# A selective-scan kernel: the last product by C of each scan run moves from GpSimd to VectorE, and TensorE adds it up ahead of turning back the first half

## The chip, the cores and the metric

The kernel runs on one core of one Trainium2 chip. A core has TensorE (PE, matmuls and transposes into PSUM; PEld is its weight load), VectorE (DVE), ScalarE (ACT), GpSimd (POOL) and SyncE (SP), which issues the transfers. Each works through its own instructions in order and waits for the others by semaphores. The metric is the device time of one execution in microseconds (us), as the median of several runs.

## The reference

Four layers run one after the other on x (2 batches, 1024 tokens, 256 channels): a linear attention (layer 0), a gated state-space block (layer 1), a bidirectional state-space block (layer 2) and a softmax attention (layer 3). The change touches the state-space scans of layers 1 and 2 alone. Each is, for 512 channels and 16 states:

```python
def step(hst, inp):
    dt_t, B_t, C_t, x_t = inp
    dA = jnp.exp(dt_t[:, :, None] * A)
    hst = hst * dA + (dt_t * x_t)[:, :, None] * B_t[:, None, :]
    y = jnp.einsum('bds,bs->bd', hst, C_t)
    return (hst, y)
```

Layer 1 has one such scan for each batch, layer 2 has one forward and one backward scan for each batch. y is then multiplied by a gate and goes through an output projection.

## The kernel before

**Runs.** The six scans are six "runs": q = 0 and 1 in layer 1 (batches 0 and 1), q = 2 to 5 in layer 2 (batch 0 forward and backward, batch 1 forward and backward). A run handles two halves of 512 tokens in turn (`r.order`), 16 states in each, 4 groups of 128 channels for each state: 128 units (`UNITS`), or 64 pairs of units (`PAIRS_N`). The pair holds two channel groups of one state: a tile `H` of 128 partitions x 1024 values, of which there are five (`HS`), used in turn.

**One pair.** TensorE forms the input u of a unit in a PSUM bank (L840 or L846). ScalarE makes the decay exp(dt*A) (L931). VectorE scans the unit with one instruction (L1000). When both units of a pair are scanned, GpSimd multiplies the pair in place by the row of C, which a transfer has spread over the partitions (L1019, semaphore `weighed`). TensorE then adds the pair into the y banks with 8 transposing matmuls (`add_up`, L865, semaphore `added`), which sums over the 16 states. The order on each engine is the order in which `run_t`, `run_s`, `run_v` and `run_p` are written.

**The end of a run.** VectorE makes its last scans of units 126 and 127. TensorE adds the pairs 61, 62 and 63. In the runs q = 0, 1, 3 and 5 the function `run_t` is given `back`, which is `turn_back_t`: `back(0)` turns the y of the first half, which has long been copied to SBUF, with 16 transposes into four banks (L1029); `back(1)` does so for the second half. VectorE multiplies each turned bank by the gate (`turn_back_v`, L1036). Between the two it takes the second half's y out of PSUM (`take_y(1)`): in q = 0 and 1 it copies the y banks 0 and 1 (L820) while ScalarE copies banks 2 and 3 (L812); in q = 3 and 5 it adds all four to the forward scan's y (L818). Each bank of `back(1)` needs all four of these parts. TensorE goes on from `back(1)` to the output projection (L265). The runs q = 2 and 4 have no `back`: TensorE goes on to the next run's inputs.

In `run_t`, `back(0)` stands between `add_up(62)` and `add_up(63)`:

```python
            for pair in range(PAIRS_N - 3, PAIRS_N):
                if pair == PAIRS_N - 1 and back:
                    back(0)
                add_up(pair)
```

Of the kernel before, what the change touches and what calls it, by code (L numbers as in the profile page):

```python
# [8 lines left out]
ALU = mybir.AluOpType  # L9
# [102 lines left out]
def program(nc, T, out):  # L112
    with ExitStack() as ctx:
# [5 lines left out]
        def sig(name, step=1):  # L119
            every.append(Sig(ctx.enter_context(nc.semaphore(name)), step))  # L120
            return every[-1]
# [35 lines left out]
        pe, act, dve, pool = sig("psum_filled"), sig("scalar_done"), sig("vector_done"), sig("pool_done")  # L157
        spread, scaled, formed = sig("b_diagonal"), sig("scaled_by_b"), sig("u_formed")
        decayed, scanned, carried = sig("decayed"), sig("scanned"), sig("carried")
        weighed, added = sig("weighed_by_c"), sig("added_up")  # L160
        taken = sig("y_taken")
        dma = {}

        def transfer(name):
            return dma[name]
# [7 lines left out]
        def area(off, *shape):  # L173
            n = 1
            for s in shape:
                n *= s
            assert off + n <= AW, (off, n)
            v = A[:, off:off + n]
            if len(shape) == 2:
                v = v.rearrange("p (a b) -> p a b", a=shape[0])  # L180
            if len(shape) == 3:
                v = v.rearrange("p (a b c) -> p a b c", a=shape[0], b=shape[1])
            return v
# [429 lines left out]
        CB = [area(WK + 7168 + 512 * j, 512) for j in range(2)]  # L613
        w2all = W2[:, 4992:7040]
        UNITS, PAIRS_N, HS = 128, 64, 5
# [109 lines left out]
        def first_state(r, j):  # L725

            return r.G[j], Bt[:, 4 * r.order[0] + j, 0:1], r.q >= 2 and j >= 2
# [23 lines left out]
        def first_copied(r, j):  # L751
            return (dve if first_state(r, j)[2] else act).at(("dut", r.q, 0, j))
# [31 lines left out]
        def second_half(w, r):  # L784

            w.wait_ge(*act.at(("dut", r.q, 1, 3)))
            w.wait_ge(*dve.at(("dut", r.q, 1, 1)))
# [15 lines left out]
        def took(r, p, j):  # L803

            return act.at(("took", r.q, p, j)) if by_scalar(r, p, j) else taken.at((r.q, p, j))

        def by_scalar(r, p, j):
            return r.n < 2 and (p == 0 or j >= 2)
# [13 lines left out]
        def run_t(e, w, r, back=None, early=None):  # L822
            q = r.q
            opened = set()

            def form_u(i):
                k, dt = divmod(i, 4)
                if k < 32:
                    ci = r.steps[k][0]
                    if ci == r.order[1]:  # L830
                        second_half(w, r)
                    if i >= 4:
                        w.wait_ge(*scanned.at((q, i - 4)))
                    else:
                        w.wait_ge(*first_copied(r, i))
                    o = PS[:, 4 + i % 4, :]
                    if k % 2:
                        w.wait_ge(*spread.at((q, k, 3)))
                        for j in range(4):
                            t = e.matmul(o[:, j * 128:(j + 1) * 128], r.DUT[:, 4 * ci + j, dt * 128:(dt + 1) * 128], DB[k // 2 % 2][:, j, :],  # L840
                                         start=True, stop=True)
                    else:
                        for j in range(4):
                            w.wait_ge(*(dve.at(("scaled", q, j)) if k == 0 and first_state(r, j)[2] else scaled.at((q, k, j))))
                        for j in range(4):
                            t = e.transpose(o[:, j * 128:(j + 1) * 128], r.G[(2 * k + j) % 6][:, dt * 128:(dt + 1) * 128], ident[:, :])  # L846
                    t.then_inc(*formed.up((q, i)))

            def open_y(ci, j):

                if (ci, j) in opened:
                    return False
                opened.add((ci, j))
                if ci == r.order[0]:
                    w.wait_ge(*(dve if j < 2 else act).at(("dut", q, 1, j)))
                else:
                    w.wait_ge(*took(r, 0, j))
                return True

            def add_up(pair):  # L860
                ci = r.steps[pair // 2][0]
                w.wait_ge(*weighed.at((q, pair)))
                for dt in (pair % 2 * 2, pair % 2 * 2 + 1):
                    for j in range(4):
                        t = e.matmul(PS[:, j, dt * 128:(dt + 1) * 128], r.H[pair % HS][:, dt % 2, j * 128:(j + 1) * 128], ident[:, :],  # L865
                                     start=open_y(ci, j), stop=True, is_transpose=True, skip_group_check=True)
                t.then_inc(*added.up((q, pair)))

            def add_skip(ci, n):
                dt, j = divmod(n, 4)  # L870
                w.wait_ge(*dve.at(("diag", q)))
                e.matmul(PS[:, j, dt * 128:(dt + 1) * 128], r.U[:, dt, ci * 512 + j * 128:ci * 512 + (j + 1) * 128], diag[:, dt, :],  # L872
                         start=open_y(ci, j), stop=True, skip_group_check=True)

            for i in range(3):
                form_u(i)
            for i in range(UNITS):
                k, dt = divmod(i, 4)
                ci, s = r.steps[k]
                if dt % 2 and i >= 7:  # L880
                    add_up((i - 7) // 2)
                form_u(i + 3)
                if 1 <= i < 5:
                    turn_du_t(e, w, r, 1, i - 1)
                if 3 <= s < 11 and dt % 2:
                    add_skip(ci, 2 * (s - 3) + dt // 2)
            banks.at, banks.held = 4, [[("last y", q, j)] for j in range(4)] + [[("last u", q, j)] for j in range(4)]
            for pair in range(PAIRS_N - 3, PAIRS_N):
                if pair == PAIRS_N - 1 and back:
                    back(0)  # L890
                add_up(pair)
                if pair == PAIRS_N - 3 and early:
                    early()
            if back:
                back(1)

        def run_s(e, w, r, y, more, early=None):
# [76 lines left out]
        def run_v(e, w, r, y, back=None):  # L974
            q = r.q

            def take_y(p):
                for j in range(4):
                    if not by_scalar(r, p, j):
                        take_v(e, w, r, p, j, y)  # L980

            for i in range(UNITS):
                k, dt = divmod(i, 4)
                ci, s = r.steps[k]
                if i == TAKEN_AT:
                    take_y(0)
                if i in (5, 6):
                    copy_du_v(e, w, r, 1, i - 5)
                if i == 6:
                    w.wait_ge(*pe.at(("dut", q, 1, 3)))  # L990
                w.wait_ge(*decayed.at((q, i)))
                w.wait_ge(*formed.at((q, i)))
                if i >= 2 * HS:
                    w.wait_ge(*added.at((q, i // 2 - HS)))
                init = 0.0
                if ci == r.order[1]:
                    w.wait_ge(*carried.at((q, 2 * s + dt // 2)))
                    init = CAR[:, 4 * s + dt:4 * s + dt + 1]
                h, a, u = (v[:, ::-1] if r.rev else v for v in (r.H[i // 2 % HS][:, dt % 2, :], A_B[i % 4], PS[:, 4 + i % 4, :]))
                e.tensor_tensor_scan(h, a, u, init, ALU.mult, ALU.add).then_inc(*scanned.up((q, i)))  # L1000
            if back:
                back(0)
            take_y(1)
            if back:
                back(1)
            for j in range(4):
                banks.give(("last y", q, j), took(r, 1, j))
                banks.give(("last u", q, j), scanned.at((q, UNITS - 4 + j)))

        def run_p(e, w, r):  # L1010
            q = r.q
            for pair in range(PAIRS_N):
                k = pair // 2
                w.wait_ge(*scanned.at((q, 2 * pair + 1)))
                if r.steps[k][0] == r.order[0]:
                    w.wait_ge(*carried.at((q, pair)))
                w.wait_ge(*transfer(f"c_load{k % 2}").at((q, k)))
                h = r.H[pair % HS]
                e.tensor_tensor(h, h, CB[k % 2].unsqueeze(1).broadcast_to([128, 2, 512]), ALU.mult).then_inc(*weighed.up((q, pair)))  # L1019
# [955 lines left out]
```

## Time and profile before

| | |
|---|---|
| median of 3 runs | 1942.12 us |
| range of these runs | 1942.08 to 1942.58 us |
| the profiled execution's own time | 1945.84 us |
| its span, first to last instruction | 1943.5 us |
| busy: PE, DVE, ACT, POOL | 95%, 82%, 73%, 54% |
| POOL's products by C (L1019) | 384 of 2396 ns mean |
| VectorE's scans (L1000) | 768 of 1201 and 1259 ns mean |
| TensorE's additions (L865) | 3072 matmuls |
| mean granted TensorE clock | 0.975 of full speed |

A granted clock of 1.00 is TensorE's level of 2.4 GHz, 0.50 is the level of 1.2 GHz. The busy shares are averages over stages with different limits, so what a change at the end of a run is worth has to be read there: in the chain of waits and in the timeline around each end. Busy time of TensorE is modelled: the matmuls overlap, and a group's end lies a little after the next group's start.

### The profile page before, as it was taken

The numbers are of one execution on the slowest core, as the hardware profiler recorded it, in microseconds if no ns is written. First come the engines' busy times: TensorE is split into PE (matmuls) and PEld (weight loads), VectorE is DVE, ScalarE is ACT, GpSimd is POOL, SyncE is SP. The second block draws the span as 40 slices with busy tenths as digits, with TensorE's granted clock in tenths as the row PEclk, the third lists the DMA queues.
The fourth block names the chain that finished last, engine by engine and source line by source line (L and its number), as shares of the span: only waits on it lengthen the run. The fifth ranks groups of instructions, "written<-read, shape, count | busy, mean of one in ns | idle before, by whom it ended". The sixth has DMA issues, their size and how long they took to land.

```text
span 1943.5 us, 32682 instructions
## 1 busy us (share of the span) xinstructions
PE 1845.3 (95%) x12312; PEld 1337.9 (69%) x12312; DVE 1600.7 (82%) x2125; ACT 1425.8 (73%) x2661; POOL 1048.6 (54%) x603
## 2 busy tenths in 40 slices
PE   6989899999999999999999999999998999999997
PEld 3664899948998599969995799689974333332323
DVE  5565899768998699989995999889987999999742
ACT  3426899468993899799974999799954377777775
POOL 3031599526994299939980699479944400003000
PEclk9989899998999999999999999999999799999999
DMA  5023111021111111101110121021101111111000
GB/s 202 1 85 99 59 57 55 32 72 43 56 59 37 51 54 60 51 24 55 56 44 2 40 60 56 24 72 58 58 15 32 38 42 38 37 37 36 17 23 22
DMA packets 57547, 95.18 MB, mean 49 GB/s; under 512 B 14951, under 2 KB 23559, under 8 KB 55982
## 3 DMA queue, kind: packets, MB, share of 16 engines
q1 hardware_dynamic: 55854, 88.90, 15.2%
q0 software_dynamic: 1536, 4.20, 0.7%
q8 instruction: 97, 1.59, 0.3%
q14 instruction: 60, 0.49, 0.1%
HBM read 73.55 MB, written 6.91 MB: 41 GB/s over the span
## 4 chain that ended last, share of the span: by engine, by line
PE 63%; POOL 14%; ACT 8%; DVE 8%; issue 6%; DMA 1%; SPq 1%; DVEq 0%; ACTq 0%; POOLq 0%
POOL A L1019 13%; PE PS L865 10%; PE PS L840 10%; PE PS L256 8%; PE PS L1603 6%; PE PS L1556 6%; PE PS L1763 5%; PE PS L846 5%; PE PS L265 3%; DVE A L1569 2%; PE PS L441 2%; PE PS L872 1%; ACT A L931 1%; ACT A L908 1%; PE PS L243 1%
## 5 line engine op out<-in xcount | busy, mean ns | idle before, releaser
L1019 POOL TENSOR_TENSOR A<-A 128x1024 f32<-128x1024 f32 x384 | 897.6, 2396 | 223.2 <-ACT small L923 111.0
L931 ACT ACTIVATE A<-A,negA 128x512 f32<-128x512 f32 x768 | 547.3, 715 | 34.0 <-DVE A L1000 24.4
L1000 DVE TENSOR_TENSOR_SCAN A<-A,PS 128x512 f32<-128x512 f32 x384 | 436.2, 1201 | 44.8 <-PE PS L846 23.8
L1000 DVE TENSOR_TENSOR_SCAN A<-A,small,PS 128x512 f32<-128x512 f32 x384 | 451.2, 1259 | 5.3 <-ACT A L931 5.3
L865 PE MATMUL PS<-ident,A 128*128 128x128 f32 x3072 | 408.5, 276 | 20.4 <-ACT A L737 13.3
L840 PE MATMUL PS<-A 128*128 128x128 f32 x3072 | 393.8, 276 | 0.9 <-ACT A L915 0.6
L865 PEld LDWEIGHTS PS<-ident,A 128*128 128x128 f32 x3072 | 352.3, 143 | 30.0 <-ACT A L737 15.9
L840 PEld LDWEIGHTS PS<-A 128*128 128x128 f32 x3072 | 368.1, 192 | 2.3 <-DVE A L1000 2.0
L1569 DVE TENSOR_REDUCE A<-PS 128x1 f32<-128x512 f32 x512 | 319.3, 681 | 38.9 <-PE PS L1556 37.3
L1800 ACT ACTIVATE A<-PS 128x512 f32<-128x512 f32 x512 | 267.2, 603 | 101.9 <-PE PS L1763 101.6
L908 ACT ACTIVATE A<-A,small 128x512 f32<-128x512 f32 x320 | 228.6, 714 | 17.3 <-PE PS L846 16.8
L846 PE MATMUL PS<-ident,A 128*128 128x128 f32 x1360 | 200.4, 279 | 4.5 <-ACT A L737 2.5
L1556 PE MATMUL PS<-A 99*128 99x512 bf16 x480 | 186.6, 397 | 13.7 <-DMA A<-scr 7.5
L256 PE MATMUL PS<-A,W 128*128 128x512 f32 (+1 forms) x416 | 184.8, 598 | 3.3 <-DVE A L766 2.9
L1763 PE MATMUL PS<-A 102*128 102x512 bf16 x480 | 178.1, 384 | 5.1 <-ACT A L1800 4.9
L846 PEld LDWEIGHTS PS<-ident,A 128*128 128x128 f32 x1360 | 162.4, 145 | 8.9 <-issue 4.1
L1534 POOL CAST W<-W 128x32 bf16<-128x32 f32 x32 | 6.7, 209 | 291.4 <-DVE W L1527 214.3
L1556 PEld LDWEIGHTS PS<-A 99*128 99x128 bf16 x480 | 46.9, 98 | 166.5 <-DVE A L1569 121.6
L230 POOL TENSOR_TENSOR RS<-VE,HALF 128x8 f32<-128x8 f32 (+1 forms) x15 | 25.7, 1712 | 248.9 <-DVE VE L225 248.9
L915 ACT ACTIVATE A<-ident,small 128x128 f32<-128x128 f32 x384 | 148.6, 393 | 0.4 <-PE PS L840 0.4
L256 PEld LDWEIGHTS PS<-A,W 128*128 128x128 f32 (+1 forms) x416 | 75.1, 185 | 102.6 <-issue 91.0
L1603 PE MATMUL PS<-A,W 128*32 128x512 f32 x1024 | 136.0, 604 | 0.0
(194 smaller groups left out, 1842.7 us busy)
## 6 DMA issues: line engine op xcount, KB each, us to landing
A<-scrc SPq DMA_DIRECT2D x192, 256.0 KB, 3.1
A<-A SPq DMA_DIRECT2D x360, 32.0 KB
scr<-A SPq DMA_DIRECT2D x4, 1024.0 KB, 4.8
W<-in_wa SPq DMA_DIRECT2D x2, 1536.0 KB, 9.7
X<-in_x SPq DMA_DIRECT2D x4, 512.0 KB, 5.3
scr<-W SPq DMA_DIRECT2D x128, 1.5 KB
out<-X SPq DMA_DIRECT2D x4, 512.0 KB, 2.9
W<-in_w SPq DMA_DIRECT2D x1, 1984.0 KB, 7.3
```

What stands on the lines that cost most here:

```text
L256: t = e.matmul(o[0:M, :], wt(k, m), act_in(k), start=k == 0, stop=k == nk - 1)
L840: t = e.matmul(o[:, j * 128:(j + 1) * 128], r.DUT[:, 4 * ci + j, dt * 128:(dt + 1) * 128], DB[k // 2 % 2][:, j, :], start=True, stop=True)
L846: t = e.transpose(o[:, j * 128:(j + 1) * 128], r.G[(2 * k + j) % 6][:, dt * 128:(dt + 1) * 128], ident[:, :])
L865: t = e.matmul(PS[:, j, dt * 128:(dt + 1) * 128], r.H[pair % HS][:, dt % 2, j * 128:(j + 1) * 128], ident[:, :], start=open_y(ci, j), stop ...
L931: e.activation(A_B[i % 4], r.DT[:, dt, ci * 512:(ci + 1) * 512], ACT.Exp, scale=negA[:, r.n, dt * 16 + s:dt * 16 + s + 1]).then_inc(*decay ...
L1000: e.tensor_tensor_scan(h, a, u, init, ALU.mult, ALU.add).then_inc(*scanned.up((q, i)))
L1019: e.tensor_tensor(h, h, CB[k % 2].unsqueeze(1).broadcast_to([128, 2, 512]), ALU.mult).then_inc(*weighed.up((q, pair)))
L1556: e.matmul(o, SQ[j][0:99, nt * 128:(nt + 1) * 128], SK3[j][0:99, c * 512:(c + 1) * 512], start=True, stop=True).then_inc(*pe.up(("trial", ...
L1569: e.tensor_reduce(NM[:, k % 2, q:q + 1], bank(("trial", k, nt, c)), AX.X, ALU.max, negate=True).then_inc(*dve.up(("trial", k, nt, c)))
L1603: t = e.matmul(PV[32 * j:32 * j + 32, c, :], V[:, tile * 272 + 17 * h:tile * 272 + 17 * h + 32], PX[mt % 2][j][:, c * 512:(c + 1) * 512], ...
L1763: e.matmul(o, SK3[sl][0:102, mt * 128:(mt + 1) * 128], SQ[sl][0:102, c * 512:(c + 1) * 512], start=True, stop=True).then_inc(*pe.up(("scor ...
L1800: e.activation(PX[mt % 2][j][:, c * 512:(c + 1) * 512], bank(key), ACT.Exp).then_inc(*act.up(("weights", u, mt, j, c)))
```

## The change

The last of the 64 products by C leaves GpSimd. VectorE makes it with the same operands right behind the scan of unit 127, in front of its own `back(0)`; it waits for its own last scan and for the transfer of that row of C, and raises a semaphore of its own (`weighed_v`), for which `add_up(63)` now waits. GpSimd makes 63 products in each run. TensorE adds pair 63 right behind pair 62, and makes `back(0)` and `back(1)` after it.

```diff
@@ add_up in run_t
-                w.wait_ge(*weighed.at((q, pair)))
+                w.wait_ge(*(weighed_v if pair == PAIRS_N - 1 else weighed).at((q, pair)))
@@ end of run_t
             for pair in range(PAIRS_N - 3, PAIRS_N):
-                if pair == PAIRS_N - 1 and back:
-                    back(0)
                 add_up(pair)
                 if pair == PAIRS_N - 3 and early:
                     early()
             if back:
+                back(0)
                 back(1)
@@ run_v, behind the loop over the units
+            w.wait_ge(*scanned.at((q, UNITS - 1)))
+            w.wait_ge(*transfer("c_load1").at((q, 31)))
+            h = r.H[(PAIRS_N - 1) % HS]
+            e.tensor_tensor(h, h, CB[1].unsqueeze(1).broadcast_to([128, 2, 512]), ALU.mult).then_inc(*weighed_v.up((q, PAIRS_N - 1)))
             if back:
                 back(0)
@@ run_p
-            for pair in range(PAIRS_N):
+            for pair in range(PAIRS_N - 1):
```

On TensorE, at the end of the run q = 0 (L865 adds pairs, L1029 turns back, and is L1032 in the changed file):

```order
 L865 MATMUL PS<-ident,A 128x128 x8
 L840 MATMUL PS<-A 128x128 x8
-L865 MATMUL PS<-ident,A 128x128 x32
-L1029 MATMUL PS<-ident,A 128x128 x16
-L865 MATMUL PS<-ident,A 128x128 x8
-L1029 MATMUL PS<-ident,A 128x128 x16
+L865 MATMUL PS<-ident,A 128x128 x40
+L1032 MATMUL PS<-ident,A 128x128 x32
```

The 8 additions of pair 63 moved from behind the first 16 transposes to in front of them; nothing else moved. The ends of q = 1, 3 and 5 have the same piece.

On VectorE, at the same place before the change (L1000 the scans, L1036 the gate, L820 the copies of y, L1219 behind the output projection):

```order
142 L1000 SCALAR_TENSOR_TENSOR A<-A,small,PS 128x512 x64
143 L1036 TENSOR_TENSOR A<-PS,A 128x512 x4
144 L820 COPY A<-PS 128x512 x2
145 L1036 TENSOR_TENSOR A<-PS,A 128x512 x4
146 L1219 TENSOR_TENSOR A<-PS,MODS 128x512 x4
```

and with it:

```order
142 L999 SCALAR_TENSOR_TENSOR A<-A,small,PS 128x512 x64
143 L1003 TENSOR_TENSOR A<-A 128x1024
144 L1039 TENSOR_TENSOR A<-PS,A 128x512 x4
145 L820 COPY A<-PS 128x512 x2
146 L1039 TENSOR_TENSOR A<-PS,A 128x512 x4
147 L1222 TENSOR_TENSOR A<-PS,MODS 128x512 x4
```

One product (L1003) stands between the last scan and the gate of the first half.

## Rows read from the trace of the kernel before

**Rows 1.** The page: shares of the chain that ended last, by engine.

```profile
PE 63%; POOL 14%; ACT 8%; DVE 8%; issue 6%; DMA 1%; SPq 1%; DVEq 0%; ACTq 0%; POOLq 0%
```

**Rows 2.** The chain, end of q = 0: start us, us, what.

```profile
363.02 2.37 POOL A L1019
...
365.43 1.09 PE PS L865 x8
...
367.00 2.48 DVE A L1036 x4
369.48 1.21 DVE A L820 x2
...
370.73 1.85 PE PS L1029 x15
372.59 13.82 PE PS L265 x64
```

**Rows 3.** Timeline, end of q = 0: start us, us, engine, line, what, [idle before <-releaser].

```profile
356.05 11.65 POOL L1019 TENSOR_TENSOR A<-A 128x1024 f32<-128x1024 f32 x5
356.90 8.28 DVE L1000 TENSOR_TENSOR_SCAN A<-A,small,PS 128x512 f32<-128x512 f32 x7
...
366.36 1.91 PE L1029 MATMUL PS<-ident,A 128*128 128x128 f32 x16
...
368.11 1.04 PE L865 MATMUL PS<-ident,A 128*128 128x128 f32 x8
...
370.13 0.33 PE L1029 MATMUL PS<-ident,A 128*128 128x128 f32 x1 [0.99 <-DVE A L820]
```

**Rows 4.** Timeline, end of q = 5.

```profile
1413.48 8.29 DVE L1000 TENSOR_TENSOR_SCAN A<-A,small,PS 128x512 f32<-128x512 f32 x7
...
1422.87 1.91 PE L1029 MATMUL PS<-ident,A 128*128 128x128 f32 x16
...
1426.72 0.33 PE L1029 MATMUL PS<-ident,A 128*128 128x128 f32 x1 [1.06 <-DVE A L818]
```

**Rows 5.** The chain, end of q = 5.

```profile
1419.51 2.39 POOL A L1019
...
1423.58 2.48 DVE A L1036 x4
...
1428.51 1.64 PE PS L1029 x13
...
1430.36 1.93 PE PS L265 x8
```

**Rows 6.** The chain, end of q = 3.

```profile
1017.65 2.54 PE PS L1029 x13
...
1020.51 2.50 PE PS L265 x8
```

**Rows 7.** Timeline, start of layer 3: VectorE's and GpSimd's products of 128x1024.

```profile
1462.46 1.22 DVE L1480 TENSOR_TENSOR A<-A 128x1024 f32<-128x1024 f32 x1
...
1465.15 2.50 POOL L1480 TENSOR_TENSOR A<-A 128x1024 f32<-128x1024 f32 x1 [5.32 <-ACT A L1470]
1465.58 3.15 DVE L1480 TENSOR_TENSOR A<-A 128x1024 f32<-128x1024 f32 x1
```

**Rows 8.** Timeline, end of q = 2.

```profile
828.44 1.29 DVE L820 COPY A<-PS 128x512 f32<-128x512 f32 x2 [4.93 <-PE PS L865]
```

**Rows 9.** Timeline, starts of q = 3 and q = 5: TensorE's longest waits there.

```profile
864.20 0.33 PE L865 MATMUL PS<-ident,A 128*128 128x128 f32 x1 [1.89 <-ACT A L737]
...
1276.22 0.33 PE L865 MATMUL PS<-ident,A 128*128 128x128 f32 x1 [1.70 <-ACT A L737]
```

**Rows 10.** Busy time by stretch: us, PE, PEld, DVE, ACT, POOL busy (count), PEclk, DMA share, GB/s.

```profile
864.60:868.00 3.40, 2.32 (x11) 2.33 (x12) 1.53 (x3) 3.25 (x7) 3.04 (x2) 0.50 0.24 82
1018.00:1021.70 3.70, 3.70 (x16) 2.97 (x15) 3.45 (x7) 0.00 (x0) 0.00 (x0) 0.54 0.00 0
```

More of the change, by code:

```diff
@@ L159, in program @@
         decayed, scanned, carried = sig("decayed"), sig("scanned"), sig("carried")
-        weighed, added = sig("weighed_by_c"), sig("added_up")
+        weighed, weighed_v, added = sig("weighed_by_c"), sig("weighed_by_c_on_vector"), sig("added_up")
         taken = sig("y_taken")
```

## The prediction

> **What bounds the kernel now.** I read the page first. The chain that ended last is 63% TensorE and 14% POOL [rows 1], and nearly all of POOL's part is the products by C inside the scan runs. That makes it tempting to think that one POOL product less in a run is 2.4 us less. The change takes only the last of 64 away, though, so what counts is which wait ends last after it. For that I read the chain in order of time around each of the six ends of a run, and then the timeline of the same stretch.
>
> At the end of q = 0 the chain goes: POOL's product of pair 62 (363.02, 2.37 us), TensorE's addition of pair 62 (365.43), the first four transposes of back(0), VectorE's four gate products of the first half (367.00 to 369.48), VectorE's two copies of y, back(1) on TensorE from 370.73, then the output projection, 64 matmuls without a gap [rows 2]. POOL's product of pair 63 is not in it. The timeline shows where that product is: POOL makes pairs 59 to 63 from 356.05 to 367.70, about 2.33 us each [rows 3]. It ends while TensorE is busy with back(0) (366.36, 16 transposes, 1.91 us). TensorE adds pair 63 from 368.11 to 369.15, and VectorE is busy with the gate products until 369.48, so it would not have looked at pair 63 earlier [rows 2, 3]. In the kernel before, both the product and the addition of pair 63 are hidden behind VectorE's gate products, with 0.33 us to spare. q = 1 repeats this. q = 3 and 5 differ only in that VectorE adds four banks instead of copying two; the chain passes through the same POOL product of pair 62 and the same gate products [rows 5].
>
> **The change part by part.**
>
> *POOL's 64th product goes* (six times). It was not on the chain at four ends. At the ends of q = 2 and 4 VectorE sits idle for 4.93 us before it takes y, and what it waits for is TensorE's addition [rows 8], which is behind the next run's first projection, not behind POOL. Worth nothing.
>
> *VectorE's product comes in* (six times). A VectorE product of 128x1024 from SBUF takes 1.22 us when POOL is quiet, and took 3.15 us when POOL's 2.50 us product, begun 0.43 us earlier, was still under way for 2.07 us [rows 7]. So a VectorE product with both operands in SBUF all but stands still while POOL works: POOL's ended at 1467.65, VectorE's at 1468.73, 1.08 us later. Here is the overlap at q = 0: the last scan ends at 365.18 [rows 3] and POOL's pair 62 at 365.39 [rows 2]. Counting 0.04 us from one instruction to the next that waits for it (POOL's end at 365.39 to TensorE's 365.43), the product would run from 365.22 to 366.44 if POOL did not matter, and to 366.61 if it stood still until POOL ends and then took its full 1.22 us. TensorE could begin adding pair 63 at 366.48 to 366.65.
>
> The Trainium skill, page "SBUF — State Buffer", section "SBUF: two separate sides", says that the port pair that VectorE and GpSimd share is an exclusive lock, held for a whole instruction by the one that starts first, also against a VectorE instruction with two SBUF inputs. The trace agrees with its 3.15 us; by that rule the upper value holds, and no more than that, because POOL has nothing behind pair 62. I lean towards the upper value.
>
> *The 8 additions of pair 63 go in front of back(0)* (four times with effect). This is the term that costs. From the addition of pair 62 to the first transpose of back(0) passes 366.36 - 365.43 = 0.93 us [rows 2, 3]; the eight additions of pair 63 will take the same. So back(0) begins at 366.48 + 0.93 = 367.41, or at 366.65 + 0.93 = 367.58, in place of 366.36: 1.05 to 1.22 us later. VectorE's first gate product needs the first four transposes, so it moves from 367.00 by the same amount, and with it the gate products, the copies, back(1) and the projection. VectorE has no slack in that stretch: the gate products, the copies and back(1) follow each other closely [rows 2].
>
> For q = 5: the last scan ends at 1421.77 [rows 4], POOL's pair 62 at 1421.90 [rows 5]. The product ends at 1423.03 to 1423.12, TensorE begins pair 63 at 1423.07 to 1423.16, back(0) at 1424.00 to 1424.09, against 1422.87 [rows 4]: 1.13 to 1.22 us later. Sum over four ends, q = 1 taken as q = 0 and q = 3 as q = 5: 2 x 1.05 + 2 x 1.13 = 4.36 to 4 x 1.22 = 4.88. I take 4.6.
>
> *What is gained by adding pair 63 early?* Its y is complete at about 367.6 instead of 369.15, and ScalarE copies its two banks earlier. VectorE stands in program order before its own gate products of the first half, however, and takes its share of y only after them. back(1) needs all four parts. So the gain is zero.
>
> *TensorE waits longer in one piece.* Before, TensorE had something to do (pair 63) while VectorE made the gate products, and its wait before back(1) was 0.99 us at q = 0 and 1.06 us at q = 5 [rows 3, 4]. After the change back(0) ends at 367.41 + 1.91 = 369.32 and back(1) begins at 370.13 + 1.05 = 371.18: a wait of 1.86 us. At q = 5 the same gives 1424.00 + 1.91 = 1425.91 to 1426.72 + 1.13 = 1427.85: 1.94 us. Elsewhere in this trace TensorE waited 1.89 and 1.70 us in one piece with single matmuls around it, at the starts of q = 3 and q = 5 [rows 9], and behind the first of these the granted clock stood at 0.50, the level of 1.2 GHz, from 864.6 to 868.0 [rows 10]. At the end of q = 3 the clock fell as it is, in the stretch from 1018.0 [rows 10], behind a wait as long as q = 5's, where it did not. What such a fall costs is the difference of those two ends: from the last 13 transposes to the end of the first eight projection matmuls q = 3 took 1020.51 + 2.50 - 1017.65 = 5.36 us and q = 5 took 1430.36 + 1.93 - 1428.51 = 3.78 us [rows 5, 6], so 1.58 us. At q = 0 the projection behind back(1) is on the chain and a fall costs about the same. At q = 1 VectorE's norm is on the chain soon after back(1), so it costs less. Of the three ends that had no fall I expect two to get one, at 1.2 us each (between 1.58 and about half of it for q = 1): 2.4 us. Bounds: no new fall, 0; all three, 3 x 1.58 = 4.7. Below zero too: q = 3 could lose its fall, since every time after 367 us shifts, for -1.6.
>
> **Sum.** In the profiled execution's time 1945.84 + 4.6 + 2.4 = 1952.8 us. That execution is 3.7 us above the median of the runs (1942.12); I know no reason for the change to alter this distance, so the forecast is 1942.12 + 7.0 = 1949.1 us.
>
> **The rivals.**
> 1. *Only the fixed term.* The waits of 1.9 us bring no net fall of the clock: +4.4 to +4.9, 1946.5 to 1947.0 us. For it: a wait of about a microsecond fell once and stayed up once, so chance plays a part. Against it: the new waits are about as long as those of rows 9.
> 2. *Within measurement.* The fixed term holds, but a fall that the kernel has now goes away: 4.6 - 1.6 = +3.0, 1945.1 us.
> 3. *Faster.* If the end of a run hung on pair 63, the earlier product would pay: POOL ends it at 367.70, VectorE would at 366.44 to 366.61, 1.1 to 1.26 us earlier, times four: 1937.1 to 1937.7 us. This decides as soon as pair 63's addition ends later than VectorE's gate products, that is, if the 0.33 us to spare were negative in the unprofiled runs. Even then the additions stand before back(0) now, so the gate products come late all the same. Little speaks for it.
> 4. *VectorE's product is much dearer.* If POOL stood in its way all through, as in the 3.15 us row, each end would cost 1.9 us more: +7.7, 1956.8 us with the forecast's terms. It needs POOL to work beside it, and POOL has at most 0.17 us left.
>
> **How the numbers follow.** Forecast (fixed term and one to three new falls, 1947.5 to 1951.8): 0.58. Rival 1: 0.24. Rival 2: 0.12. Rival 3: 0.03. Rival 4: 0.03. A measurement of this kernel can tell about 0.2%, 3.9 us, from no change; 1946.0 us is that bound. Slower: 0.58 + 0.24 + 0.03 = 0.85. Within: 0.12. Faster: 0.03. The range leaves out rivals 3 and 4 and the edge of the rest: 1945.3 to 1951.9 us.
>
> **What would show it.** In the changed kernel's timeline at q = 0: VectorE's 128x1024 product right behind the last scan, 1.2 to 1.4 us long; TensorE's additions of pairs 62 and 63 with 0.1 to 0.3 us between them; the first gate product 1.0 to 1.25 us after where it stood, measured from POOL's end of pair 62 (before: 367.00 - 365.39 = 1.61 us, after: 2.7 to 2.8 us); TensorE's wait before back(1) near 1.9 us in place of 0.99; a granted clock of 0.50 in the projection at some of the four ends. At q = 2 and 4 nothing moves. I am wrong if the distance from POOL's pair 62 to the projection's first matmul has not grown by 1.0 to 1.3 us at each of the four ends, or if the clock stays at 1.00 at all of them.

## The result and the profile after

The changed kernel takes 1951.96 us (median of 10 runs, 1948.60 to 1954.78), the kernel before 1945.20 us (median of 10 runs, 1942.08 to 1948.26, the three runs known beforehand among them). The ratio is 1.0038, with a 95% interval of 1.0027 to 1.0050: slower by 6.8 us in the medians and by 7.4 us by the ratio. The forecast was slower by 7.0 us, from 1942.12 to 1949.1, with a range of 1945.3 to 1951.9 us. The measured time lies just above that range.

The profiled execution has a span of 1950.0 us against 1943.5 us, and a mean granted clock of 0.973 against 0.975. The chain in order of time at the end of q = 0 (start us, us, what), to be laid beside [rows 2]:

```profile
363.13 2.37 POOL A L1022
...
365.55 2.17 PE PS L865 x16
...
368.19 2.48 DVE A L1039 x4
370.68 1.21 DVE A L820 x2
...
371.93 2.39 PE PS L1032 x15
374.32 5.90 PE PS L265 x22
```

TensorE's addition of pair 62 begins at nearly the same time as before (365.55 against 365.43), but it is now 16 matmuls in one piece, pairs 62 and 63. VectorE's gate products begin at 368.19, 2.64 us after the addition began; before it was 367.00 - 365.43 = 1.57 us. Each step behind them is as late. The timeline of the same stretch, beside [rows 3] (with the idle time before a row in brackets):

```profile
365.32 1.25 DVE L1003 TENSOR_TENSOR A<-A 128x1024 f32<-128x1024 f32 x1
365.55 2.17 PE L865 MATMUL PS<-ident,A 128*128 128x128 f32 x16 [0.53 <-POOL A L1022]
367.56 1.91 PE L1032 MATMUL PS<-ident,A 128*128 128x128 f32 x16
...
371.33 0.33 PE L1032 MATMUL PS<-ident,A 128*128 128x128 f32 x1 [1.86 <-DVE A L820]
371.93 2.39 PE L1032 MATMUL PS<-ident,A 128*128 128x128 f32 x15 [0.27 <-DVE A L820]
```

back(0) (L1032) begins 367.56 - 365.55 = 2.01 us after the addition of pair 62, before 0.93 us: 1.08 us later. TensorE's wait before back(1) is 1.86 us, before 0.99. The 15 transposes behind it took 2.39 us, before 1.85 [rows 2]: the clock fell in them. The busy time by stretch (us, then PE, PEld, DVE, ACT, POOL busy with counts, granted clock, DMA share, GB/s), behind the four ends q = 0, 1, 3 and 5:

```profile
373.20:376.50 3.30, 3.30 (x12) 2.83 (x11) 1.85 (x4) 0.00 (x0) 0.00 (x0) 0.50 0.00 0
612.10:615.40 3.30, 3.30 (x13) 2.93 (x11) 3.20 (x8) 0.00 (x0) 0.00 (x0) 0.50 0.00 0
1018.00:1021.70 3.70, 2.67 (x17) 1.91 (x17) 3.21 (x7) 0.00 (x0) 0.00 (x0) 1.00 0.00 0
1431.30:1434.60 3.30, 3.08 (x14) 2.63 (x13) 2.40 (x4) 0.00 (x0) 0.00 (x0) 0.50 0.00 0
```

Three ends ran at 1.2 GHz for a while, and q = 3, which had fallen before [rows 10], stayed at 2.4 GHz. Its chain, and that of q = 5, changed places against [rows 5, 6]. End of q = 3:

```profile
1020.01 1.64 PE PS L1032 x13
...
1021.86 1.92 PE PS L265 x8
```

End of q = 5:

```profile
1431.68 3.03 PE PS L1032 x13
```

**Where the 6.5 us of the span lie.** I cut both traces at the same events: the first addition of pair 62, the first matmul of the projection behind back(1), and the first transpose (L243) behind the projection.

| us | before | changed | difference |
|---|---|---|---|
| start to pair 62 of q = 0 | 365.43 | 365.55 | +0.12 |
| end of q = 0, projection | 6.99 + 13.82 | 8.56 + 15.01 | +2.76 |
| to pair 62 of q = 1 | 215.82 | 215.51 | -0.31 |
| end of q = 1, projection | 7.00 + 14.32 | 8.71 + 14.86 | +2.25 |
| to pair 62 of q = 3 | 387.71 | 384.11 | -3.60 |
| end of q = 3, projection | 9.03 + 17.67 | 9.27 + 16.98 | -0.45 |
| to pair 62 of q = 5 | 384.15 | 385.42 | +1.27 |
| end of q = 5, projection | 8.14 + 16.98 | 10.67 + 16.98 | +2.53 |
| the rest | 496.44 | 498.37 | +1.93 |

The first number of each end runs from pair 62 to the projection, the second to the transpose behind it. The four ends together are +7.1 us, all else -0.6 us. The stretches between differ by up to 3.6 us although their instructions are the same but for the products that moved: at 680 us, for one, before had a fall of the clock and the changed kernel had none.

### The profile page after: what moved, and what is told of

The parts are those of the page before. It is cut to its first block, busy times and chain, and to the rows that moved or that the text cites. A ratio compares the mean times of both kernels' runs of the same rounds, so it can differ in the third digit from the quotient of the medians.

```text
span 1950.0 us, 32688 instructions
## 1 busy us (share of the span) xinstructions
PE 1850.5 (95%) x12312; PEld 1339.7 (69%) x12312; DVE 1608.0 (82%) x2131; ACT 1426.0 (73%) x2661; POOL 1036.5 (53%) x597
## 4 chain that ended last, share of the span: by engine, by line
PE 70%; ACT 9%; POOL 8%; DVE 8%; issue 4%; DMA 1%; SPq 1%; DVEq 0%; ACTq 0%; POOLq 0%
PE PS L865 13%; PE PS L840 12%; POOL A L1022 7%; PE PS L256 7%; PE PS L1606 6%; PE PS L846 6%; PE PS L1559 6%; PE PS L1766 5%; PE PS L265 4%; DVE A L1572 2%; PE PS L872 2%; ACT A L930 2%; PE PS L441 2%; ACT A L907 1%; ACT A L1803 1%
## 5 line engine op out<-in xcount | busy, mean ns | idle before, releaser
L1022 POOL TENSOR_TENSOR A<-A 128x1024 f32<-128x1024 f32 x378 | 883.5, 2390 | 220.8 <-ACT small L922 108.5
L865 PE MATMUL PS<-ident,A 128*128 128x128 f32 x3072 | 407.9, 276 | 20.6 <-ACT A L737 13.3
L865 PEld LDWEIGHTS PS<-ident,A 128*128 128x128 f32 x3072 | 351.6, 142 | 30.8 <-ACT A L737 15.7
```

## The experiments

Every kernel was run in turn with the kernel before on the same chip, experiments 1 to 4 on one chip and 5 to 7 on another, so two changed kernels are compared through the kernel before. "The end" is the stretch from the first addition of pair 62 to the first matmul of the projection. Because falls of the clock come and go from run to run, I also compare at equal clock: each run has its mean granted clock, and a fit with one common slope and one offset for each kernel, through all 112 runs of these nine kernels that have one (-1.16 us for each 0.001 of clock), gives each kernel an offset from the kernel before. For the changed kernel it is +4.0 us (95%: 3.0 to 5.0); its mean clock is 0.9728 against 0.9758, which is worth another 3.5 us. The two make up the difference of the means, 1952.2 - 1944.7 = 7.5 us.

**1. TensorE's order as before, the product on VectorE.**

```diff
             for pair in range(PAIRS_N - 3, PAIRS_N):
+                if pair == PAIRS_N - 1 and back:
+                    back(0)
                 add_up(pair)
...
             if back:
-                back(0)
                 back(1)
```

> The changed kernel with TensorE's order as it was: back(0) stands between the additions of pairs 62 and 63 again, VectorE keeps the last product. Theory (the cost lies in the eight additions ahead of back(0) and in the longer wait of TensorE that follows): VectorE's product ends at about 366.5 at q = 0, before its first gate product could begin at 367.0, so it is hidden. The time is that of the kernel before, within 0.1% (ratio 0.999 to 1.001), the distance from POOL's end of pair 62 to the first gate product is 1.6 us again, and TensorE's wait before back(1) is 1.0 us. Rival (VectorE's added product is what costs, 1.2 us at each of six ends or more through the port it shares with GpSimd): +5 to +7 us, ratio 1.003 or more.

Measured: 1944.52 us, ratio 0.9996 (0.9985 to 1.0008), at equal clock -0.1 us (-0.9 to +0.8), mean clock 0.9765. Its timeline at q = 0:

```profile
362.64 1.25 DVE L1004 TENSOR_TENSOR A<-A 128x1024 f32<-128x1024 f32 x1
362.87 1.09 PE L865 MATMUL PS<-ident,A 128*128 128x128 f32 x8 [0.52 <-POOL A L1023]
363.80 1.91 PE L1033 MATMUL PS<-ident,A 128*128 128x128 f32 x16
364.43 2.48 DVE L1040 TENSOR_TENSOR A<-PS,A 128x512 f32<-128x512 f32 x4 [0.54 <-PE PS L1033]
```

VectorE still sits idle for 0.54 us between its product and the gate products, and these begin 364.43 - 362.87 = 1.56 us after the addition of pair 62, as before the change. The product on VectorE costs nothing that these runs can tell; TensorE's order is the cause. The clock fell here at q = 3 and at q = 5, although TensorE's wait before back(1) was 1.06 us there as before the change, where only q = 3 fell:

```profile
1015.90:1019.20 3.30, 3.30 (x13) 2.57 (x12) 3.14 (x7) 0.00 (x0) 0.00 (x0) 0.50 0.01 2
1425.50:1428.80 3.30, 3.17 (x14) 2.77 (x14) 2.41 (x4) 0.00 (x0) 0.00 (x0) 0.50 0.00 0
```

**2. TensorE's order alone**, in the kernel before, with GpSimd keeping the last product (the edit is the reverse of the diff above, applied to the kernel before).

> The kernel before with only the additions of pair 63 moved ahead of back(0); GpSimd keeps all 64 products. Theory: TensorE now waits for GpSimd's product of pair 63, which ends 2.3 us after that of pair 62, so back(0) begins about 2.3 us later at four ends: +9.3 us fixed, plus falls of the clock, +10 to +14 us in all (ratio 1.005 to 1.007). Rival (the order costs nothing, the product on VectorE does): ratio 1.000.

Measured: 1957.21 us, ratio 1.0062 (1.0049 to 1.0075), at equal clock +10.4 us (9.1 to 11.6). The timeline at q = 0:

```profile
364.38 1.09 PE L865 MATMUL PS<-ident,A 128*128 128x128 f32 x8 [0.49 <-POOL A L1018]
366.69 1.09 PE L865 MATMUL PS<-ident,A 128*128 128x128 f32 x8 [1.21 <-POOL A L1018]
367.61 1.91 PE L1028 MATMUL PS<-ident,A 128*128 128x128 f32 x16
```

back(0) begins 367.61 - 364.38 = 3.23 us after the addition of pair 62, against 0.93: 2.3 us later, of which 1.21 us is TensorE waiting for GpSimd. It is 2.3 us at q = 1 and 5 too, and 2.9 us at q = 3, where the clock fell already in the additions and in back(0). So moving the product to VectorE is worth 1.2 us at each end, but only once the order has put that product in the way.

**3. VectorE takes y first**, in the changed kernel.

```diff
+            take_y(1)
             if back:
                 back(0)
-            take_y(1)
-            if back:
                 back(1)
```

> The changed kernel with VectorE taking the second half's y before it makes the gate products of the first half. Theory: y is complete at about 367.6 at q = 0, VectorE takes it while TensorE makes back(0), back(1) follows back(0) without a wait of 1.9 us, and the projection can begin when the first half's gate products are done, about 0.9 us earlier than in the kernel before at each of four ends. -3.6 us fixed against the kernel before and fewer falls of the clock at the ends: ratio 0.997 to 0.9985. Rival (VectorE's added product holds the ends up whatever the order): no faster than the kernel before, ratio 1.000 to 1.004.

Measured: 1941.14 us, ratio 0.9975 (0.9964 to 0.9985): faster than both kernels. At equal clock -2.1 us (-3.1 to -1.2), mean clock 0.9773, the highest of all. The timeline at q = 0:

```profile
365.38 2.17 PE L865 MATMUL PS<-ident,A 128*128 128x128 f32 x16 [0.54 <-POOL A L1021]
367.40 3.66 PE L1031 MATMUL PS<-ident,A 128*128 128x128 f32 x32
...
367.60 1.29 DVE L820 COPY A<-PS 128x512 f32<-128x512 f32 x2 [1.19 <-PE PS L865]
368.80 4.86 DVE L1038 TENSOR_TENSOR A<-PS,A 128x512 f32<-128x512 f32 x8
371.33 8.90 PE L265 MATMUL PS<-W,A 128*128 128x256 f32 x40 [0.28 <-DVE A L1038]
```

back(0) and back(1) are now 32 transposes in one piece, and the projection begins 371.33 - 365.38 = 5.95 us after the addition of pair 62, before 6.99. The other ends have 5.95, 7.30 and 7.20 us, for 7.00, 9.03 (with a fall) and 8.14; none of the four had a fall. The gain is smaller than forecast, -2.1 and not -3.6 us. About 0.8 us of the difference is explained: at q = 1 the chain does not go through the projection: VectorE's norm follows its last gate product, and VectorE's work is no shorter. From the addition of pair 62 to the first transpose behind the projection that end has 21.24 us, before 21.32. The other three are 0.9 us shorter each (q = 3 set against q = 5 before, which had no fall), so the traces give -2.8 us for the four ends.

**4. A shorter wait of TensorE, nothing else.** In the changed kernel, eight transposes of old data into a bank that VectorE has read already, between back(0) and back(1); nobody reads their result.

```diff
                 back(0)
+                fill()
                 back(1)
```

> The changed kernel with eight more transposes, whose result nobody reads, between back(0) and back(1), so that TensorE's wait of 1.9 us is cut to about 1 us; nothing on the chain moves. Theory (4.4 us of the loss are fixed and the rest are falls of the clock that follow the longer wait): fewer falls at the four ends, about +4.4 us against the kernel before, ratio 1.0015 to 1.003, with the distance from POOL's end of pair 62 to the first gate product still 2.7 us. Rival (the clock has nothing to do with the wait; all 7.3 us are fixed): ratio 1.0038, as the changed kernel.

Measured: 1952.61 us, ratio 1.0035 (1.0023 to 1.0047). The ratio is nearer to the rival's, and its interval takes in both. The profile shows what the edit did and did not do:

```profile
373.00:376.00 3.00, 3.00 (x16) 2.64 (x15) 1.28 (x3) 0.00 (x0) 0.00 (x0) 1.00 0.00 0
1021.20:1024.40 3.20, 3.03 (x14) 2.64 (x13) 2.31 (x4) 0.00 (x0) 0.00 (x0) 0.50 0.00 0
1434.20:1437.40 3.20, 3.03 (x14) 2.64 (x13) 2.31 (x4) 0.00 (x0) 0.00 (x0) 0.50 0.00 0
```

q = 0 and q = 1 had no fall, with ends of 8.08 and 8.08 us: 1.09 and 1.08 us longer than before, the fixed term without the clock. q = 3 and q = 5 fell all the same: there a wait of 1.06 us is left, and behind it single transposes with 0.27 us between them. The mean clock was 0.9735, the offset at equal clock +4.6 us (3.6 to 5.7). The edit was too weak for q = 3 and 5. It also shows something that the theory does not explain. Outside the four ends this profile stood at 1.2 GHz for 106 us, the profile before for 92 us and the changed kernel's for 96 us, in stretches that the edit does not touch.

**5. No long wait at all.** As 4, with 14 transposes, and two more behind each of the first parts of back(1)'s first bank.

```diff
-                for n in range(8):
+                for n in range(14):
...
+                    if p == 1 and m == 0 and j < (3 if r.n == 2 else 1):
+                        for n in range(2):
+                            e.transpose(PS[:, banks.place.get(("back", r.q, 0, 0), 4), n * 128:(n + 1) * 128], r.H[(PAIRS_N - 1) % HS][:, 0, n * 128:(n + 1) * 128], ident[:, :])
```

> The changed kernel with 14 transposes whose result nobody reads between back(0) and back(1), and two more behind each early part of back(1)'s first bank, so that TensorE's longest wait at the four ends is about 0.4 us. Theory (a fixed 4.4 us, and falls of the clock at the ends for the rest): the ends last 8.1, 8.1, 9.3 and 9.3 us from the addition of pair 62 to the projection, no fall of the clock at any of them; the mean granted clock is back near 0.975 to 0.976 and the time 4 to 5.5 us above the kernel before, ratio 1.002 to 1.003. Rival (the falls are a matter of the runs' starts and layer 3, not of these waits): the ends lose their falls but the mean clock stays near 0.973 and the time at +7 us, ratio 1.0038.

Measured: 1949.02 us, ratio 1.0027 (1.0013 to 1.0041), mean clock 0.9756. TensorE's longest wait at q = 0 (at q = 3 and 5 it is 0.40 us), and the four ends:

```profile
370.00 0.33 PE L1038 MATMUL PS<-ident,A 128*128 128x128 f32 x1 [0.34 <-DVE A L820]
```

```profile
364.00:380.00 16.00, 15.41 (x100) 13.80 (x101) 8.68 (x13) 1.09 (x2) 0.15 (x1) 1.00 0.01 1
603.00:625.00 22.00, 21.09 (x127) 18.73 (x127) 18.35 (x39) 1.09 (x2) 1.70 (x2) 1.00 0.00 1
1012.00:1040.00 28.00, 27.21 (x150) 20.90 (x151) 23.94 (x53) 2.34 (x4) 1.64 (x1) 1.00 0.00 1
1422.00:1440.00 18.00, 17.01 (x104) 13.43 (x104) 13.96 (x37) 9.30 (x3) 1.97 (x2) 1.00 0.00 1
```

All four ends stayed at 2.4 GHz and lasted 8.09, 8.08, 9.26 and 9.27 us. The offset at equal clock is +4.4 us (3.4 to 5.4), the mean clock about that of the kernel before (0.9758). More work on TensorE, with none of it used, took the falls away at the ends. The median is 2.9 us lower than the changed kernel's (1951.96 and 1949.02), but the intervals of the two ratios overlap, so a gain in time is likely and not shown. In the profile the four ends, up to the transpose behind the projection, last 4.3 us less than in the changed kernel's.

**6. VectorE takes y first, GpSimd keeps the last product** (experiment 3 with the product back in `run_p`).

> The version in which VectorE takes y first, but with GpSimd keeping the last product. Theory: the addition of pair 63 waits for GpSimd until 2.3 us after that of pair 62, so each end is about 1.1 us longer than with the product on VectorE: about 7.1, 7.1, 8.3 and 8.3 us from the addition of pair 62 to the projection, where the kernel before has 7.0, 7.0, 9.0 (with a fall) and 8.1. Time within 0.1% of the kernel before, ratio 0.999 to 1.001. Rival (the gain of the version with y first comes from the order alone and the engine of the product does not matter): ratio 0.9975.

Measured: 1948.37 us, ratio 1.0016 (1.0004 to 1.0028), at equal clock +2.9 us (2.0 to 3.7). The ends last 7.17, 7.17, 8.46 and 8.37 us, as expected, 1.2 us longer than in experiment 3, but the time is worse than I had written (a ratio of at most 1.001). The chain at q = 1 shows what I had left out:

```profile
609.59 1.11 PE PS L865 x8
...
610.72 1.29 DVE A L820 x2
612.00 2.24 DVE A L1034 x4
...
614.31 2.47 DVE A L1034 x4
616.78 2.59 DVE W L1086 x8
```

VectorE's work is the chain there from the addition of pair 63 through both halves' gate products to the norm (L1086), so the whole wait for GpSimd is on it: 7.17 + 15.27 = 22.44 us up to the transposes behind the projection, before 21.32. VectorE's product is worth having: with this order it is 1.2 us an end.

**7. The suspected cost twice.** In the changed kernel, eight transposes of no use between the addition of pair 63 and back(0).

```diff
             if back:
+                w.wait_ge(*scanned.at((q, UNITS - 4)))
+                for n in range(8):
+                    e.transpose(PS[:, 4, n % 4 * 128:(n % 4 + 1) * 128], r.H[(PAIRS_N - 1) % HS][:, 0, n % 4 * 128:(n % 4 + 1) * 128], ident[:, :])
                 back(0)
                 back(1)
```

> The changed kernel with eight more transposes, whose result nobody reads, between the addition of pair 63 and back(0): the suspected cost twice. Theory (each transpose ahead of back(0) delays VectorE's gate products and all behind them in full, 0.87 us for eight): the ends grow by 0.87 us each, +3.5 us against the changed kernel, ratio 1.005 to 1.0065 against the kernel before. Rival (the ends have slack for them): ratio 1.0038.

Measured: 1955.70 us, ratio 1.0064 (1.0051 to 1.0077), at equal clock +8.6 us (7.4 to 9.8), about twice the changed kernel's offset. The timeline at q = 0:

```profile
365.57 2.18 PE L865 MATMUL PS<-ident,A 128*128 128x128 f32 x16 [0.58 <-POOL A L1025]
367.59 1.04 PE L895 MATMUL PS<-ident,A 128*128 128x128 f32 x8
...
368.46 1.91 PE L1035 MATMUL PS<-ident,A 128*128 128x128 f32 x16
369.10 2.48 DVE L1042 TENSOR_TENSOR A<-PS,A 128x512 f32<-128x512 f32 x4 [2.50 <-PE PS L1035]
```

The gate products begin 369.10 - 365.57 = 3.53 us after the addition of pair 62: 1.57 before, 2.64 changed, 3.53 here. The eight transposes are delay in full: 0.89 us here, 3.6 us for four ends, and 4.6 us by the offsets, whose intervals allow both. All four ends had a fall.

## Why the prediction missed its range, and what of it was right

The step that failed is the base to which the sum was added: the kernel before has a median of 1945.20 us over ten runs, 3.1 us above the 1942.12 us that I took. It is worked out under "The number" below. The mechanism of the fixed term held; that of the clock term held at two of the four ends.

**What bounds.** Right. Pair 63 was not on the chain; with its product and its addition hidden, the chain through VectorE's gate products could only be hurt. Experiment 1 gives the old time back with VectorE's product in place.

**GpSimd's 64th product goes, VectorE's comes in: nothing.** Right for both, by experiment 1. At q = 2 and 4 the stretch did not change: VectorE waits 3.60 us (before 4.93) for TensorE's addition, shorter by its own product of 1.32 us. The product took 1.25 us at q = 0 with GpSimd at work for 0.17 us of it. I had leaned towards the upper value, 1.22 us counted from GpSimd's end; the row lies at the lower one. Here are all six, by line:

```profile
L1003 DVE TENSOR_TENSOR A<-A 128x1024 f32<-128x1024 f32 x6 | 7.6, 1266 | 0.2
```

The Trainium skill's rule of the exclusive lock ("SBUF — State Buffer", "SBUF: two separate sides") would have given 0.17 + 1.22 = 1.39 us for q = 0, and 2.07 + 1.22 = 3.29 us for the row of 3.15 us. Both are 0.14 us too long. The six products overlap GpSimd's last one by 0.17, 0.20, 0.23, 0.09, 0.22 and 0.09 us and took 1.25, 1.28, 1.32, 1.23, 1.30 and 1.23 us. So all of them, and the row of 3.15 us, fit one reading: VectorE's product stands still until 0.14 us before the recorded end of GpSimd's, and then takes 1.22 us.

**The additions ahead of back(0): 1.05 to 1.22 us at each end.** Right. Without a fall of the clock the ends are longer by 1.09 (q = 0, experiment 4), 1.08 (q = 1) and 9.27 - 8.14 = 1.13 us (q = 5 before against q = 3 changed, neither with a fall). q = 3 and q = 5 in experiment 5 confirm it with 9.26 and 9.27. The sum is 2.17 + 2.26 = 4.4 us, forecast 4.6, and the measures at equal clock agree: +4.0 for the changed kernel and +4.4 for experiment 5. My own sign for it was badly set. I had asked that each end grow by 1.0 to 1.3 us up to the projection, and in the profile they grew by 1.57, 1.71, 0.24 and 2.53 us, because the clock falls already in back(1). Only without the falls are the growths 1.09, 1.08 and 1.13 us.

**The longer wait and the clock: 2.4 us.** Right in size, and in mechanism only at q = 0 and 1. The waits were 1.86 us at q = 0 and 1 and 1.93 us at q = 3 and 5, forecast 1.86 and 1.94. In the profiled execution three ends fell and q = 3 lost its fall. Against the same ends of experiment 4 without a fall, q = 0 paid (8.56 + 15.01) - (8.08 + 13.81) = 1.68 us and q = 1 (8.71 + 14.86) - (8.08 + 14.32) = 1.17 us; q = 5 paid 10.67 - 9.27 = 1.40 us, and q = 3 gave back 1.58 us. That is 2.7 us. All profiles that have a wait of TensorE before back(1), side by side (its length in us, then the ends that fell):

| | q = 0 and 1 | fell | q = 3 and 5 | fell |
|---|---|---|---|---|
| before | 0.99 | none | 1.06 | q = 3 |
| experiment 1 | 0.99 | none | 1.06 | both |
| experiment 4 | 0.99 | none | 1.06 | both |
| changed | 1.86 | both | 1.93 | q = 5 |
| experiment 2 | 1.86, 1.87 | both | 1.54, 1.93 | q = 3 |
| experiment 7 | 1.87, 1.86 | both | 1.93 | both |
| experiment 5 | 0.34 | none | 0.40 | none |

At q = 0 and 1 the longer wait decides: no fall in six ends with 0.99 us, a fall in all six with 1.86 us or a little more. At q = 3 and 5 it does not: five of six ends fell with 1.06 us and four of six with the longer waits. There the old wait was long enough already, with the single transposes behind it. That the profile before had only one fall of these two, and the changed one the other, is chance as far as these profiles tell; so the net count of two falls came out right in part by luck.

Over all the runs the lower mean clock is worth 3.5 us (3.0 thousandths at 1.16 us each). Only a part of that is shown to come from the ends. Experiment 4 had no fall at q = 0 and 1, yet its mean clock, 0.9735, is nearer to the changed kernel's than to that of the kernel before, 0.9758. Experiment 5 has no wait over 0.4 us at the ends, and its mean clock, 0.9756, is back; but its ends lost the falls of q = 3 and 5 too, so it should have risen above, as in experiment 3 (0.9773). What moves the falls outside the ends stays open.

**The rivals.** "Only the fixed term", +4.4 to +4.9 us, lies below the lower end of the measured interval (0.0027 of 1945.2 us is 5.3 us). Experiment 5 turned the kernel into it (+3.7 us on the median, +5.3 us by the ratio). "Faster" failed as its condition said: pair 63 had to be late for VectorE, and it was not. The dear product did not appear.

**The number.** The measured 1951.96 us is 2.9 us above the forecast and 0.06 us above the top of my range, 1951.9. The shift, 6.8 us in the medians and 7.4 us by the ratio, lies on either side of the 7.0 us of the sum. The step that failed is the one that carried the sum over to the base: "1942.12 + 7.0". I took the median of three runs that lie within 0.5 us of each other as the kernel's time, and put the profiled execution, 3.7 us above them, down as something the change would not alter. The three were among the lowest: over ten runs the median is 1945.20, over the 24 and 19 runs beside the experiments 1944.60 and 1945.35, and single runs span 1939.65 to 1949.36. With 1945.2 as the base the same sum gives 1952.2. The profile had a warning in it: its page shows the granted clock under nine tenths in four of 40 slices, and a single fall was priced at 1.58 us in the prediction itself, so three nearly equal runs do not bound what a fourth will do. The range should have been some 3 us wider on either side for it. Its top does not follow from the terms either: 1942.12 + 4.88 + 4.7 is 1951.7.

## What to carry to other kernels

Work that fills an engine's wait on the chain's own engine is not free to be moved ahead of what the chain needs, even when its input is made earlier: ask in whose program order the result is taken next, and move that first (experiment 3 is the change's idea with the consumer moved too, and it wins). And a delay that turns a TensorE wait of 1 us into one of 1.9 us can cost twice, once as delay and once in what the clock does to the matmuls behind it: here it did at two ends of four (1.68 and 1.17 us), and the other two fell about as often without it. When single runs differ by more than the change is worth, compare them at equal clock and end by end, and take no base from three runs. One profile of each kernel is not enough to count falls: it showed one of q = 3 and 5 falling before, where the next one showed both.

## What the runs showed of the hardware

- Matmuls whose results are thrown away took the falls of the clock away at the four ends (experiment 5), and the mean granted clock over the runs was 0.9756 against 0.9728 in the changed kernel. A gain in time, 2.9 us between the medians, is likely and not shown.
- A TensorE wait of 1.06 us followed by three single transposes 0.27 us apart was followed by a fall of the clock at five of six ends (q = 3 and 5 before and in experiments 1 and 4). A wait of 0.99 us followed by one such gap was not, at any of the six ends with that pattern (q = 0 and 1, the same profiles). With 1.86 us in place of 0.99 all six fell (changed, experiments 2 and 7).
- Which stretches of the same instructions run at 1.2 GHz differs from profile to profile (at 680 us before, and not in the changed kernel), and stretches of some 385 us differed by up to 3.6 us.
- A VectorE product of 128x1024 with both inputs in SBUF stood still while GpSimd's product ran, until 0.14 us before the recorded end of that one: 1.22 us alone, 1.25 us with 0.17 us of overlap, 1.32 us with 0.23 us, 3.15 us with 2.07 us.
